# Keys and values projected as paired half steps in a two-layer cross-attention kernel, with new orders of work

## The reference

```python
x = x + L0_xattn(layernorm(x), ctx)       # 16 heads of 16, q = x @ Wq, k = ctx @ Wk, v = ctx @ Wv, softmax, @ Wo
x = x + L0_ffn(layernorm(x))              # one of 8 experts per token, with a capacity; 256 -> 1024 -> 256
x = x + L1_xattn(layernorm(x), ctx)       # the same with biases, then relu(out @ W1 + b1) @ W2 + b2
x = x + L1_ffn(layernorm(x))              # a cell of 6 nodes, each an attention of 8 heads over the sequence
```

## Time and profile before

| what | value |
|---|---|
| median of three runs | 4048.85 us |
| the profiled execution's own time | 4048.74 us |
| its span | 4046.9 us |
| busy PE / PE weight loads / ACT / DVE / POOL | 3974.8 / 3397.6 / 2651.8 / 2400.2 / 1865.0 us |
| HBM traffic over the span | 33 GB/s |

### The profile page before, as it was taken

One profiled execution on the slowest core, in us unless ns is written; L12 is line 12 of the kernel. 1 busy time (PEld: TensorE's weight loads), 2 busy tenths in 40 slices (PEclk: granted clock), 3 DMA queues, 4 the chain that ended last, 5 costly groups with the idle time before them and its releaser, 6 DMA issues.

```text
span 4046.9 us, 100880 instructions
## 1 busy us (share of the span) xinstructions
PE 3974.8 (98%) x38276; PEld 3397.6 (84%) x38276; DVE 2400.2 (59%) x6216; ACT 2651.8 (66%) x11851; POOL 1865.0 (46%) x1979
## 2 busy tenths in 40 slices
...
DMA packets 117867, 129.74 MB, mean 32 GB/s; under 512 B 12006, under 2 KB 110676, under 8 KB 117264
## 3 DMA queue, kind: packets, MB, share of 16 engines
...
## 4 chain that ended last, share of the span: by engine, by line
PE 76%; DVE 1%; ACT 0%; POOL 0%; issue 0%; DMA 0%; POOLq 0%
PE c_product L1552 37%; PE c_product L1563 15%; PE c_product L1611 10%; PE c_scores L1601 7%; PE c_product L1634 5%; PE c_product L1622 2%; DVE c_qT L1407 1%; PE c_product L1540 1%; ACT c_front_probs L1364 0%; PE c_product L1671 0%; DMA out<-c_fin 0%; POOL c_fin L1348 0%; DVE c_nodes L1407 0%; POOL c_front_probs L1318 0%; ACT c_probsT L1370 0%
## 5 line engine op out<-in xcount | busy, mean ns | idle before, releaser
L1318 POOL TENSOR_TENSOR c_probs<-c_probs,c_row_inv 128x512 f32<-128x512 f32 x744 | 770.3, 1045 | 1357.0 <-DVE c_row_inv L1419 1351.4
L1364 ACT ACTIVATE c_probs<-c_scores,c_neg_max 128x128 f32<-128x128 f32 x2976 | 1052.6, 407 | 333.1 <-DVE c_neg_max L1416 332.9
L1552 PE MATMUL c_product<-c_nodes,cell_w 128*128 128x256 f32 x4352 | 1065.2, 383 | 2.8 <-DVE c_nodes L1478 2.4
L1552 PEld LDWEIGHTS c_product<-c_nodes,cell_w 128*128 128x128 f32 x4352 | 796.2, 190 | 121.4 <-DVE c_nodes L1407 8.3
L1416 DVE TENSOR_REDUCE c_neg_max<-c_scores 128x4 f32<-128x512 f32 x1024 | 658.9, 680 | 177.6 <-PE c_scores L1601 170.1
L1364 ACT ACTIVATION_READ_ACCUMULATOR c_probs<-c_scores,c_neg_max 128x1 f32 x2976 | 733.1, 246 | 0.0
L1370 ACT COPY c_probsT<-c_product 128x512 f32<-128x512 f32 x744 | 408.1, 602 | 433.9 <-PE c_product L1611 430.4
L1364 ACT ACTIVATE c_front_probs<-c_scores,c_neg_max 128x128 f32<-128x128 f32 x1120 | 399.6, 398 | 182.5 <-DVE c_neg_max L1416 182.5
L1563 PE MATMUL c_product<-cell_w,c_nodes 128*128 128x256 f32 x1792 | 429.3, 379 | 0.0
L1318 POOL TENSOR_TENSOR c_front_probs<-c_front_probs,c_row_inv 128x512 f32<-128x512 f32 x280 | 295.0, 1057 | 291.0 <-DVE c_row_inv L1419 289.3
L474 ACT ACTIVATE a_probs<-a_scores,a_neg_max 128x128 f32<-128x128 f32 x1024 | 360.4, 409 | 47.4 <-DVE a_neg_max L545 47.0
...
## 6 DMA issues: line engine op xcount, KB each, us to landing
...
```

Source lines behind the costliest of these rows:

```text
L1318: nc.gpsimd.tensor_tensor(e, e, rinv[:, i, r].unsqueeze(2).broadcast_to([P, 4, T]), ALU.mult).then_inc(norm_made, 1)
L1364: a = nc.scalar.activation(probs(n, j)[:, r, k], S[r][:, k], ACT.Exp, bias=nmax[:, i, r, k:k + 1], accum_out=rsum[:, i, r, k:k + 1])
L1552: i = T_.matmul(m[:, u], w[:, k, u * P:(u + 1) * P], src[:, k], start=n == 0, stop=n == last)
```

## The change

The context is laid out with its last 64 rows twice (rows 128 to 191 and again as 192 to 255). The keys' weights have zeros in the last 64 rows, the values' weights have zeros in rows 128 to 191 and their own last 64 rows behind them. Where K is followed at once by V (of the job before in the first layer, of the same job in the second), the K step does only its two full-height calls, and the V step does its two full-height calls and then four calls of 64 rows: two for K on rows 0 to 63, two for V on rows 64 to 127, in turn, into two different banks. Where they don't stand so, both steps are as before. In addition the cyclic orders, heads and tails of all four engines are new in both layers; the first layer gets an ACT tail, which it had not. The rows and context of job 1 are loaded behind fused load 11 (before: 13 and 15).

```diff
 FIRST_PE_ORDER = """
-Tn:6 Q:1 T0.1:3 T1.1:3 S0:1 A:3 r.n:7 K:0 O:3 T1.0:2 T0.0:2 S1:1 L:6 Tx:0 V:1
+T0.1:3 T1.1:3 S0:1 A:3 Tn:5 Tx:0 O:3 r.n:6 T0.0:2 T1.0:2 S1:1 K:0 V:1 Q:0 L:5
 """
 FIRST_DVE_ORDER = """
-O^:3 S1.i3:2 st1:3 S0.i1:1 S0.i3:1 S0.i0:1 S0.i2:1 S1.x3:1 S1.x2:1 S1.x1:1 Tx^:0 L^:6 S1.x0:1 r.sh:6 V^:1
-Tn^:5 Q^:0 r.oh:6 S1.i1:1 S1.i0:1 st:-1 S0.x2:0 S0.x0:0 S0.x3:0 A^:2 r.n^:6 S1.i2:1 S0.x1:0 mk:-2 K^:-1
+S0.i0:2 S1.i1:2 mk:0 K^:1 V^:2 Q^:1 L^:6 st:0 r.sh:6 S1.i0:2 S1.i2:2 S0.i2:2 S0.x0:1 r.oh:6 S0.x1:1 S0.x2:1
+A^:3 S1.i3:2 Tn^:5 S0.x3:1 Tx^:0 O^:3 S0.i1:1 st1:3 r.n^:6 S0.i3:1 S1.x1:1 S1.x2:1 S1.x0:1 S1.x3:1
 """
 FIRST_ACT_ORDER = """
-nm:-1 T0^1:1 S1.e3:0 S1.e2:0 S1.e1:0 r.ex:5 S1.e0:0 T0^3:1 T0^2:1 T1^3:1 T1^2:1 S0.e2:-1 S0.e3:-1 S0.e0:-1
-S0.e1:-1 T1^0:0 T1^1:0 T0^0:0
+T1^2:3 r.ex:6 nm:0 S0.e0:1 S0.e2:1 S0.e1:1 S0.e3:1 T0^0:2 T0^1:2 T1^0:2 T1^1:2 S1.e1:1 S1.e2:1 S1.e3:1 S1.e0:1
+T0^3:2 T0^2:2 T1^3:2
 """
 FIRST_POOL_ORDER = """
-S0.n3:2 nm1:4 put:11 S0.n1:2 S1.n0:2 rs:0 S0.n2:2 S1.n1:2 S0.n0:2 S1.n2:2 S1.n3:2 rs1:3
+S0.n2:3 rs1:4 nm1:4 S0.n0:2 put:10 rs:0 S1.n0:2 S1.n2:2 S0.n1:2 S1.n1:2 S0.n3:2 S1.n3:2
 """
...
 FIRST_PE_HEAD = """
-K:0 Tx:0 Q:0 S0:0 Tx:1 V:0 K:1 Q:1 S1:0 Tx:2 K:2 S0:1 V:1 T0.0:0 T1.0:0 S1:1 Q:2 T0.1:0 T1.1:0 S0:2 A:0 V:2
...
+K:0 Tx:0 Q:0 K:1 S0:0 Tx:1 V:0 Q:1 S1:0 Tx:2 S0:1 Q:2 T1.0:0 T0.0:0 S1:1 K:2 V:1 T0.1:0 T1.1:0 S0:2 Tx:3 A:0
...
 FIRST_PE_TAIL = """
-F0:1 B0:1 A:2 O:2 T1.0:1 T0.0:1 L:5 Tn:4 T0.1:1 T1.1:1 F1:1 B1:1 A:1 r.n:5 O:1 L:4 Tn:3 L:3 Tn:2 L:2 Tn:1 r.n:3
-L:1 F2:1 B2:1 r.n:1 F3:1 B3:1 F4:1 B4:1 F5:1 B5:1
+L:7 T0.0:4 T1.0:4 S1:3 K:2 V:3 Tn:6 Q:2 T0.1:4 T1.1:4 S0:2 A:4 L:6 K:1 V:2 T0.0:3 S1:2 Tn:5 Tx:1 O:4 L:5
+T1.0:3 Q:1 T0.1:3 S0:1 T1.1:3 F0:1 A:3 T0.0:2 r.n:5 B0:1 Tn:4 S1:1 T1.0:2 O:3 T0.1:2 T1.1:2 V:1 A:2 T0.0:1 O:2
+T0.1:1 T1.0:1 L:4 T1.1:1 Tn:3 A:1 L:3 O:1 Tn:2 F1:1 r.n:3 L:2 Tn:1 L:1 B1:1 F2:1 r.n:1 B2:1 F3:1 B3:1 F4:1
+F5:1 B4:1 B5:1
 """
...
-            for n, j in on_pe:
+            keys_m = None
+            half = slice(0, P // 2), slice(P // 2, P)
+
+            for (n, j), after in zip(on_pe, on_pe[1:] + [None]):
...
-                    project(product(n, j), wk, ct[:, o]).then_inc(prod, 1)
+                    if after != ("V", j - 1):
+                        project(product(n, j), wk, ct[:, o]).then_inc(prod, 1)
+                    else:
+                        keys_m = product(n, j)
+                        for u in range(2):
+                            T_.matmul(keys_m[:, u], wk[:, 0, u * P:(u + 1) * P], ct[:, o, 0], start=u == 0, stop=False)
...
-                    project_rows(product(n, j), wv, ct[:, o]).then_inc(prod, 1)
+                    m = product(n, j)
+                    if keys_m is None:
+                        project_rows(m, wv, ct[:, o]).then_inc(prod, 1)
+                    else:
+
+                        for b in range(PAIR):
+                            T_.matmul(m[:, b], ct[:, o, 0, b * T:(b + 1) * T], wv[:, 0], start=b == 0, stop=False)
+                        for u in range(2):
+                            k = T_.matmul(keys_m[:, u], wk[half[0], 1, u * P:(u + 1) * P], ct[half[0], 1 - o, 1], start=False, stop=u == 1)
+                            v = T_.matmul(m[:, u], ct[half[1], o, 1, u * T:(u + 1) * T], wv[half[1], 1], start=False, stop=u == 1)
+                        k.then_inc(prod, 1)
+                        v.then_inc(prod, 1)
+                        keys_m = None
...
 PE_ORDER = """
-O4:2 f.Ab1:0 Q5:2 f.W1a:0 f.W1b:0 f.Tx:-1 f.W2:0 T2.0:1 S5:2 T2.1:1 V2:1 f.Q:-1 f.Txn:0 V5:2 Q0:0 K0:0 A2:1
-S0:0 O2:1 K3:1 T5.0:2 Q3:1 T5.1:2 V0:0 T0.0:0 S3:1 A5:2 f.K:-1 T0.1:0 O5:2 K1:0 T3.0:1 A0:0 f.Sb0:-1 O0:0 V3:1
-T3.1:1 Q1:0 f.Tb0.0:-1 K4:1 A3:1 S1:0 O3:1 V1:0 Q4:1 T1.0:0 S4:1 T1.1:0 K5:1 f.V:-1 f.Tb0.1:-1 V4:1 A1:0
-f.Sb1:-1 f.Ab0:-1 O1:0 T4.0:1 K2:0 T4.1:1 Q2:0 f.Tb1.0:-1 A4:1 S2:0 f.Tb1.1:-1
+O4:2 f.Tx:-1 f.Ab1:0 Q5:2 f.W1a:0 f.W1b:0 S5:2 f.W2:0 f.Q:-1 T2.0:1 V5:2 T2.1:1 K3:1 f.Txn:0 V2:1 K0:0 Q0:0
+T5.0:2 A2:1 S0:0 O2:1 V0:0 T5.1:2 Q3:1 T0.0:0 A5:2 S3:1 f.K:-1 f.V:-1 O5:2 T0.1:0 K1:0 T3.0:1 A0:0 f.Sb0:-1
+O0:0 V3:1 T3.1:1 Q1:0 K4:1 S1:0 A3:1 f.Tb0.0:-1 O3:1 V1:0 T1.0:0 Q4:1 T1.1:0 S4:1 A1:0 f.Tb0.1:-1 K5:1 O1:0
+f.Sb1:-1 f.Ab0:-1 V4:1 T4.0:1 K2:0 T4.1:1 Q2:0 f.Tb1.0:-1 A4:1 S2:0 f.Tb1.1:-1
 """
...
 PE_HEAD = """
-F6:0 F7:0 B6:0 B7:0 F8:0 B8:0 F9:0 B9:0 F10:0 F11:0 f.Tx:0 f.K:0 f.Q:0 f.Sb0:0 B10:0 F12:0 F13:0 f.Tb0.0:0
...
+F6:0 F7:0 B6:0 B7:0 F8:0 f.Tx:0 f.K:0 f.V:0 f.Q:0 F9:0 f.Sb0:0 F10:0 B8:0 B9:0 B10:0 F11:0 f.Tb0.0:0 f.Tb0.1:0
...
-SECOND_ROWS_BEHIND, SECOND_CONTEXT_BEHIND = 13, 15
+SECOND_ROWS_BEHIND, SECOND_CONTEXT_BEHIND = 11, 11
...
-    arrays["ctx_pairsT"] = whole_tiles(c.reshape(-1, PAIR, *c.shape[1:]).transpose(0, 3, 1, 2).reshape(
-        c.shape[0] // PAIR, c.shape[2], PAIR * c.shape[1]), 1)
-    for n in ("L0_xattn_Wk", "L0_xattn_Wv", "L1_xattn_Wk", "L1_xattn_Wv"):
-        arrays[n + "_rows"] = whole_tiles(arrays.pop(n), 0)
+    c = c.reshape(-1, PAIR, *c.shape[1:]).transpose(0, 3, 1, 2).reshape(c.shape[0] // PAIR, c.shape[2], PAIR * c.shape[1])
+    arrays["ctx_pairsT"] = np.ascontiguousarray(np.concatenate([c, c[:, P:]], 1))
+    for n in ("L0_xattn", "L1_xattn"):
+        wk, wv = arrays.pop(n + "_Wk"), arrays.pop(n + "_Wv")
+        gap = np.zeros_like(wk[P:])
+        arrays[n + "_Wk_rows"] = np.concatenate([wk, gap])
+        arrays[n + "_Wv_rows"] = np.concatenate([wv[:P], gap, wv[P:]])
```

More of the change, by code:

```diff
@@ L178 @@
 """
 FIRST_POOL_TAIL = """
-put:8 rs1:1 nm1:1 put:7 put:6 put:5 put:4 put:3 put:2 put:1
+put:11 S0.n2:3 S0.n3:3 put:10 S1.n3:3 S0.n0:3 S0.n1:3 rs:1 S1.n0:3 S0.n1:2 S1.n2:3 S1.n1:3 S0.n2:2 put:9
+S1.n3:2 S0.n0:2 rs1:4 S0.n3:2 nm1:4 S1.n0:2 S1.n2:2 S1.n1:2 S0.n2:1 S0.n0:1 S0.n3:1 put:8 S0.n1:1 rs1:3 nm1:3
+S1.n1:1 S1.n0:1 S1.n3:1 S1.n2:1 put:7 rs1:2 nm1:2 put:6 rs1:1 nm1:1 put:5 put:4 put:3 put:2 put:1
+"""
+FIRST_ACT_TAIL = """
+S1.e0:3 S1.e3:3 T0^3:4 T1^3:4 T0^2:4 T1^2:4 S0.e2:2 S0.e0:2 S0.e3:2 S0.e1:2 T0^1:3 nm:1 T0^0:3 S1.e0:2 S1.e2:2
@@ L221, in phase_first_layer @@
         (FIRST_PE_HEAD, on_pe), (FIRST_DVE_HEAD, on_dve), (FIRST_ACT_HEAD, on_act), (FIRST_POOL_HEAD, on_pool)))
-    on_pe, on_dve, on_pool = (ended(tail, order, JOBS) for tail, order in (
-        (FIRST_PE_TAIL, on_pe), (FIRST_DVE_TAIL, on_dve), (FIRST_POOL_TAIL, on_pool)))
+    on_pe, on_dve, on_act, on_pool = (ended(tail, order, JOBS) for tail, order in (
+        (FIRST_PE_TAIL, on_pe), (FIRST_DVE_TAIL, on_dve), (FIRST_ACT_TAIL, on_act), (FIRST_POOL_TAIL, on_pool)))
     def is_turn(n):
@@ L1012 @@
[L1012 to L1015 removed]
+f.Sb0.e2:0 f.Sb0.e1:0 f.Sb0.e0:0 f.Sb0.e3:0 f.Tb0^0:0 f.Tb0^3:0 f.Tb0^1:0 f.Tb0^2:0 f.Sb1.e0:0 f.Sb1.e1:0
@@ L1016 @@
+S3.e1:1 T0^3:2 T0^2:2 S3.e2:1 T3^0:1 f.Sb0.e1:3 f.Sb0.e0:3 T3^1:1 f.Sb0.e3:3 V3^:1 T3^2:1 f.Sb0.e2:3
 """
 DVE_HEAD = """
-F6^:0 F7^:0 B7^:0 F8^:0 B6^:0 f.x2:0 f.st:0 B8^:0 F9^:0 B9^:0 f.x:0 F11^:0 f.Tx^:0 F10^:0 f.K^:0 f.Q^:0
-f.Sb0.x0:0 f.Sb0.x1:0 f.Sb0.x2:0 f.Sb0.i0:0 f.Sb0.x3:0 B10^:0 f.Sb0.i2:0 F12^:0 f.Sb0.i1:0 F13^:0 f.Sb0.i3:0
-f.x2:1 f.st:1 f.Sb1.x2:0 f.Sb1.x1:0 f.Sb1.x0:0 f.Sb1.i2:0 f.Sb1.x3:0 B11^:0 f.Sb1.i0:0 f.V^:0 f.Sb1.i1:0
-F14^:0 B13^:0 B12^:0 f.Sb1.i3:0 f.Ab0^:0 f.x:1 F15^:0 f.Ab1^:0 f.W1a^:0 f.Tx^:1 f.W1b^:0 f.W2^:0 f.st3:0
```

317 lines of the change are left out of this document (171 added, 146 removed).

## The result

The changed kernel takes 4061.01 us (median of ten runs, 4057.69 to 4062.44), the kernel before 4049.16 beside it: the ratio is 1.0027, 95% interval [1.0018, 1.0036]. It is slower by 0.27%, where 0.66% faster was forecast (4022). Its profiled execution has a span of 4059.2 us.

A forecast was written before the change was run, and what follows sets the result against it. PE was taken to bound the kernel (busy 3974.8 of 4046.9 us). Pairs -28.1, other orders 0, layer one's cycle +6, its ends -2.5, layer two's cycle +2, its ends -4 sum to -26.6: 4022 us, range 4010 to 4040.

The forecast's parts named there:

- The pair: K and V projections in both layers: half calls side by side save 0.46 us a pair, 61 pairs, -28.1 us.
- (b): Rival, in each pair: the halves run one after the other, +24.7 in place of -28.1, 4073 us; chance 0.06.
- (c): Rival, in each pair: halves overlap only in steps, five record slots, 13 us less gain, 4035 us; chance 0.05.
- Layer two: Pairs there 32 x 0.46; its cycle's new order +2 us (0.07 x 29), its head with the tail -4.
- f.Tx: Head of layer two: this PE step may wait for the front rows, up to some 2 us.
- Layer one's cycle: Layer one's repeating jobs: the new order gives back +6 us (0 to +12), from 1.0 per four jobs.
- r.oh ahead of A^: Layer one's routing jobs: one-hot chain on DVE takes 4.1 us, leaving PE idle 4.1 ahead of O.
- the ring of x: Layer one's ordinary jobs: POOL's ring through SP's load of x holds them at 16.7 us, not 16.4.
- POOL's rs idle for about 1 us: Sign in layer one: POOL's rs stands behind DVE's mean, idle ahead of it about 1 us.
- Heads and tails of layer one: Start and end of layer one: new orders bring -2.5 us (-8 to +4) beside the pairs.
- F0's wait: Tail of layer one: F0's wait of 2.7 us for a bank goes.
- (a): Rival: ring holds all ordinary jobs, r.oh costs its 4.1, layer two's order adds 0.3 a job; 4037 us; chance 0.18.

The follow-up runs named there:

- experiment 3: Changed kernel with all its orders, but K and V always as four full calls each, no pairs: 4081.80 us, ratio 1.0066.
- Experiment 6: Changed kernel, but in layer one's routing jobs POOL's five products S.n wait until the one-hot chain r.oh is done: 4043.89 us, ratio 0.9982.
- experiment 5: Changed kernel, but PE repeats Tx's four transposes 11 more times in six routing jobs, filling its wait ahead of O: 4047.54 us, ratio 0.9993.
- experiments 9 and 10: Kernel with the one-hot chain in two, jobs 8 to 27: POOL normalises one of two row tiles (4020.26 us); ACT's copy T1^3 moves 128 of 512 columns (4022.48).
- experiment 7: Changed kernel with layer one's one-hot chain r.oh cut in two, at two places on DVE, r.n^ and put moved: 4021.14 us, ratio 0.9928.
- experiment 8: Kernel with the one-hot chain in two, but layer one's heads and tails of the kernel before: 4030.29 us, ratio 0.9947.

## Why the prediction was wrong

**The pair: its price right, where it shows half right.** 0.46 was worked out (3.46 - 2.99 is 0.47, a slip without weight); the trace shows 2.98 instead of 3.46 us, experiment 3 shows 0.47 in layer two's period. The strips of 64 rows pay the tolls of those of 32. Rivals (b) and (c) are refuted; (b) would have been 4075 by its own terms, not 4073. But "nothing hides it: PE's own queue is the chain" holds for layer two alone: in layer one some 1.1 of 1.84 us a set come through, by experiment 3; which waits take up the rest wasn't tested.

**Layer two: right.** -0.57 a job against -0.40 forecast: the order adds no wait at all (one of 0.16 ahead of S4 stands in both traces) and brings another 0.1. With the ends, -15.5 against -14.7 + 2 - 4 = -16.7. f.Tx did wait for the front rows, 1.99 us, as forecast.

**Layer one's cycle: the step that failed.** Forecast: +6 beside the pairs, thus -0.8 for each set of four jobs. Measured: +4.9 a set (26.9 over 22 jobs). The place was named, r.oh ahead of A^ and PE idle ahead of O; its price was wrong in three ways.
- The chain was priced at 4.1 us from the earlier trace rows, where POOL had nothing to do behind the chain's third instruction. In the new orders five products of POOL run beside it, and the chain takes 5.8. The wait was 5.4 instead of 4.1. Experiment 6 shows the cause, and its size: without the overlap the chain is back at 4.1. The Trainium skill (SBUF — State Buffer, SBUF: two separate sides) states that a DVE instruction with two SBUF inputs and a GpSimd instruction that reads SBUF take the same port pair as an exclusive lock for a whole instruction each; by that rule, the ends 0.08 us behind each of POOL's products agree. That DVE's instructions hold POOL up in their turn isn't seen: POOL's products keep their 1.00 us. It wasn't weighed in the prediction, nor was a hint in the trace of the kernel before: the chain's L619, beside POOL's last product, has a mean of 552 ns there, its likes behind it 225 to 248.
- The clock was held to be 1.00 throughout; the sum has no term for it. The wait of 5.4 us was followed by 1.2 GHz for the whole of O, in all six routing jobs: +1.8 each (24.90 against 23.13 in experiment 5, which shows it).
- The queues behind the late maxima (T1.0, S1 and K wait 0.5 to 0.7 each) were left out: about 1 us.

Together these are 4.1 of the 5.7 us between forecast and measurement. Another 1.2 are the three ordinary jobs, which take 16.61, 16.75 and 17.13 and not the 16.43 (16.89 - 0.46) on which the sum stood. Of the rest, 0.4, the wait of 1.57 us without a shown cause is 0.3 (once in 5.5 sets).

**What bounds an ordinary job: half right.** 16.7 was about the size, but by the ring of x; experiments 9 and 10, both on the kernel of experiment 7, take the ring off the path and put ACT on it, of which the prediction said that it decides nothing alone. That the size came out near 16.7 was luck. The sign it named, POOL's rs idle for about 1 us, did appear (0.97 at 225.90), and shows by itself nothing of what PE waits for.

**Heads and tails of layer one: wrong in sign.** -2.5 was forecast beside the pairs. Measured, with seven pairs in them (-3.2): +1.4 and +2.2, so about +7 instead of -2.5. F0's wait is gone as forecast; r.n:27 and r.n:29 wait instead (3.7 and 2.5). Yet the old ends on the new cycle are 9 us worse (experiment 8). The tables of the ends aren't the flaw, the clock is a large part: the same tail is 6.8 us shorter in experiment 5, where the stretch at half level from 632 us on is broken up. What makes that stretch long in one run of the tail and short in another stays open, and so does the head.

**The sum.** -26.6 was forecast, the spans differ by +12.3. Of these 39 us the 22 jobs between S1 of job 7 and of job 29 hold 31 (5.5 sets by 5.7), the ends of layer one about 9, layer two 1, and the experts' phase gives 3 back, with the clock of its first 7 us. None of the rivals held either of the two costs that decided, the products of POOL beside the chain and the clock behind the wait: the nearest, (a), ended at 4037, and the chance of a slower kernel was laid on (b) and on layer two, where nothing went wrong.
